# A perceiver layer with cross attention, gated linear attention and experts: one first norm instead of two, head norms by square root and reciprocal, weight splits three blocks ahead, and the turns of self attention ahead of the next scores

## The reference, cut to what matters

```python
def _ln(x, w, b):
    mu = jnp.mean(x, axis=-1, keepdims=True)
    var = jnp.mean(jnp.square(x - mu), axis=-1, keepdims=True)
    return (x - mu) * jax.lax.rsqrt(var + EPS) * w + b          # EPS = 1e-05

def _fp8_linear_pertensor(x, wq, w_scale, in_scale):
    xq = _div_clamp_fp8(x, in_scale)          # clip, bfloat16, then fp8 e4m3
    return jnp.einsum('bsi,oi->bso', xq * in_scale, wq) * w_scale

# x: (8, 64, 512); 16 heads of queries, 8 of keys and values, 128 wide
x1 = _layernorm(x)                            # (x - mean) / sqrt(var + 1e-5)
ln_out = _ln(x1, ln_w, ln_b)
q  = _ln(_fp8_linear_pertensor(ln_out, wq,  wq_scale,  q_in_scale).reshape(b, s, g, hpg, d), qln_w, qln_b)
qx = _ln(_fp8_linear_pertensor(ln_out, wqx, wqx_scale, qx_in_scale).reshape(b, s, g, hpg, d), qxln_w, qxln_b)
k  = _ln(_fp8_linear_pertensor(ln_out, wk,  wk_scale,  k_in_scale).reshape(b, s, g, d), kln_w, kln_b)
v  = _fp8_linear_pertensor(ln_out, wv, wv_scale, v_in_scale).reshape(b, s, g, d)
core = _gqa(q, k, v)                          # self attention, 64 positions a batch
# then cross attention of qx with 1601 context rows a batch, the output
# projection, x = x + ...; a gated delta-rule attention layer; a mixture of
# experts: none of them is touched by the change
```

## Time and profile before

| | before |
|---|---|
| median of 3 runs | 3088.67 us (3081.49 to 3090.84) |
| profiled execution | 3089.42 us |
| its span, first to last instruction | 3087.6 us |
| TensorE busy, share of the span | 2750.4 us, 89% |
| DVE busy | 1848.7 us, 60% |
| ACT busy | 1502.0 us, 49% |
| POOL busy | 535.5 us, 17% |
| TensorE busy in the first 320 us | 201.2 us, 63% |
| TensorE busy, 320 to 900 us | 560.0 us, 97% |

### The profile page before, as it was taken

One profiled execution on the slowest core, in us unless ns is written; L12 is line 12 of the kernel. 1 busy time (PEld: TensorE's weight loads), 2 busy tenths in 40 slices (PEclk: granted clock), 3 DMA queues, 4 the chain that ended last, 5 costly groups with the idle time before them and its releaser, 6 DMA issues.

```text
span 3087.6 us, 38294 instructions
## 1 busy us (share of the span) xinstructions
PE 2750.4 (89%) x13446; PEld 2223.8 (72%) x13446; DVE 1848.7 (60%) x4678; ACT 1502.0 (49%) x2880; POOL 535.5 (17%) x359
## 2 busy tenths in 40 slices
PE   4667999999999999999999999677998878886999
PEld 3556777778778687787787777555876778765887
DVE  6843744735636437446365373476858867466997
ACT  3652533524434326235244252233676466855776
POOL 3530200201102002011010020133333222102111
PEclk8886999999999999999999999878999989997999
DMA  2333401102003012021020020332666553418996
GB/s 85 96 89 111 120 2 48 51 4 70 27 9 89 4 38 61 4 62 35 5 87 11 22 66 3 127 109 75 164 179 167 161 124 76 141 69 337 380 374 242
DMA packets 246877, 303.06 MB, mean 98 GB/s; under 512 B 143896, under 2 KB 165016, under 8 KB 233376
## 3 DMA queue, kind: packets, MB, share of 16 engines
q1 hardware_dynamic: 243888, 296.36, 30.2%
q0 software_dynamic: 2800, 4.27, 0.6%
HBM read 259.48 MB, written 46.98 MB: 99 GB/s over the span
## 4 chain that ended last, share of the span: by engine, by line
PE 68%; DVE 16%; ACT 7%; issue 3%; DMA 2%; POOL 2%; SPq 2%; POOLq 0%; ACTq 0%; DVEq 0%
PE ps L103 17%; PE ps L105 16%; PE ps L104 16%; PE ps L690 5%; PE ps L707 3%; PE ps L672 2%; PE ps L737 2%; DVE tq L1138 2%; DVE lnw L787 1%; DVE lnw L1835 1%; DVE zz L1838 1%; POOL rs L345 1%; DVE cv L1802 1%; PE ps L728 1%; ACT pr L908 1%
## 5 line engine op out<-in xcount | busy, mean ns | idle before, releaser
L1017 POOL TENSOR_TENSOR lnw<-lnw,half 128x8 f32<-128x8 f32 (+1 forms) x104 | 170.7, 1642 | 1464.9 <-DVE lnw L792 1464.9
L103 PE MATMUL ps<-whf,cth 128*128 128x512 f32 (+1 forms) x832 | 340.1, 409 | 8.2 <-DVE ctl L509 4.8
L103 PE MATMUL ps<-cnh,pth 128*128 128x512 f32 (+1 forms) x832 | 331.3, 398 | 13.7 <-ACT kn L908 13.7
L105 PE MATMUL ps<-whf,ctl 128*128 128x512 f32 (+1 forms) x832 | 329.7, 396 | 0.0
L104 PE MATMUL ps<-wlf,cth 128*128 128x512 f32 (+1 forms) x832 | 329.2, 396 | 0.0
L105 PE MATMUL ps<-cnh,ptl 128*128 128x512 f32 (+1 forms) x832 | 325.3, 391 | 0.0
L104 PE MATMUL ps<-cnl,pth 128*128 128x512 f32 (+1 forms) x832 | 325.0, 391 | 0.0
L898 DVE TENSOR_SCALAR pc<-ps,sm 128x512 f32<-128x512 f32 x64 | 48.1, 751 | 318.2 <-PE ps L105 318.2
L2275 DVE TENSOR_TENSOR ml<-mr,mh 128x2048 fp32r<-128x2048 f32 x90 | 203.5, 2288 | 34.5 <-ACT mh L2219 34.5
L908 ACT ACTIVATE pr<-ps,lnw 128x128 f32<-128x128 f32 (+1 forms) x384 | 144.5, 457 | 162.0 <-DVE lnw L811 162.0
L939 ACT ACTIVATE pr<-ps,sm 128x1601 f32<-128x1601 f32 x64 | 102.6, 1603 | 247.4 <-DVE sm L831 217.3
(11 more groups left out here) (315 smaller groups left out, 6305.8 us busy)
## 6 DMA issues: line engine op xcount, KB each, us to landing
mr<-in_moe SPq DMA_DIRECT2D x90, 1024.0 KB, 7.2
ctr<-in_ctxt SPq DMA_DIRECT2D x96, 256.0 KB, 2.9
pr<-in_ctxn SPq DMA_DIRECT2D x96, 256.0 KB
wr<-in_wqkv SPq DMA_DIRECT2D x64, 256.0 KB, 2.9
wvf<-in_wattn SPq DMA_DIRECT2D x12, 1024.0 KB, 4.9
ca<-cat_d SPq DMA_DIRECT2D x8, 1024.0 KB, 5.7
pw<-in_wproj SPq DMA_DIRECT2D x8, 1024.0 KB, 8.3
qk_d<-cv SPq DMA_DIRECT2D x32, 256.0 KB, 3.2
```

Source lines behind the costliest of these rows:

```text
L103: pe.matmul(dst, lh, rh, start=first, stop=False)
L105: return pe.matmul(dst, ll, rh, start=False, stop=last)
L1017: po.tensor_tensor(rs[0:w, s, :], nv[0:w, s, :], half[0:w, 0:8], ALU.pow).then_inc(kx_rs, 1)
```

## The change

- The two first norms become one. The variance v of x goes to `nv` as v(1 + 1e-5) + 1e-10, whose power of minus one half is the product of both scalings; the second pass is no longer made.
- Head norms: ACT takes the square root of `nv1` (with a bias of 1e-5 from a new tile `eps5`) into `rs1`, DVE its reciprocal. POOL has no part in it.
- `split_weight_ac` becomes `scale_weight_ac` and `split_weight_ac`; both work for block j+3 in iteration j, where they were for j+2, and the scaling and the split stand on either side of ACT's half of `qn`. POOL's remainder is four instructions of 128x512. POOL's first split waits for the applied norm, its second for the first quantized input.
- Quantizing: `quantize_x_dv` moves behind DVE's half of `qn`, and `quantize_x_ac` from the start to the end of ACT's iteration.
- `project_pe` waits for the heads of block j-2 bank by bank instead of for all four.
- Self attention: TensorE turns pair i before the scores of pair i+1 (they came after), DVE computes the sums of pair i+1 before it copies pair i, and ACT copies `pT` of pair i before the exponent of pair i+1.

```diff
--- before.py
+++ after.py
@@ -140,6 +140,7 @@
         pT = sb1("pT", [128, 8, 128])
         am = sb1("am", [128, 2, 16])
         asum = sb1("asum", [128, 2, 16])
+        eps5 = sb1("eps5", [128, 1])
         s1.close()
 
         d_w, d_qx = sems("d_w", 2), sems("d_qx", 4)
@@ -174,7 +175,8 @@
                         sp.dma_start(qx_d[:, :, hd // 2, hd % 2, :].rearrange("b p s -> p b s"),
                                      qxs[:, n % 4, :].rearrange("p (b s) -> p b s", b=NB)).then_inc(d_qx[n % 4], 16)
 
-        def layer_norm_dv(dv, n):
+        def layer_norm_dv(dv):
+
 
             for i in range(4):
                 t = vs(dv.bn_stats(bns[:, i, 0, :], x0[:, i, :]))
@@ -182,8 +184,8 @@
                 dv.wait_ge(dv_step, t - 3 + i)
                 t2 = vs(dv.bn_aggr(mv[:, i, 0, :], bns[:, i, 0, :]))
             dv.wait_ge(dv_step, t2)
-            dv.tensor_scalar(nv[:, :, 0], mv[:, :, 0, 1], 1e-5, None, ALU.add).then_inc(ln_var, 1)
-            dv.wait_ge(ln_rs, n + 1)
+            dv.tensor_scalar(nv[:, :, 0], mv[:, :, 0, 1], 1.0 + 1e-5, 1e-10, ALU.mult, ALU.add).then_inc(ln_var, 1)
+            dv.wait_ge(ln_rs, 1)
             for i in range(4):
                 dv.tensor_scalar(x0[:, i, :], x0[:, i, :], mv[:, i, 0, 0:1], rs[:, i, 0:1],
                                  ALU.subtract, ALU.mult).then_inc(ln_done, 1)
@@ -212,10 +214,9 @@
         def s1_dv(dv):
             dv.memset(half[:, :], -0.5).then_inc(consts_set, 1)
             dv.memset(eps6[:, :], 1e-6).then_inc(consts_set, 1)
+            dv.memset(eps5[:, :], 1e-5).then_inc(consts_set, 1)
             dv.wait_ge(d_x, 16)
-            layer_norm_dv(dv, 0)
-            dv.wait_ge(ln_done, 4)
-            layer_norm_dv(dv, 1)
+            layer_norm_dv(dv)
             dv.wait_ge(d_vec, 16)
             for c in range(4):
                 dv.wait_ge(x_turned, c + 1)
@@ -241,13 +242,10 @@
                     for m in range(16):
                         tb = vs(dv.bn_aggr(mv1[:, s, m, :], bn1[:, s, m, :]))
                     dv.wait_ge(dv_step, tb)
-                    tb = vs(dv.tensor_scalar(nv1[:, s, :], mv1[:, s, :, 1], wsc, wsc, ALU.mult, ALU.mult))
+                    dv.tensor_scalar(nv1[:, s, :], mv1[:, s, :, 1], wsc, wsc, ALU.mult, ALU.mult).then_inc(hn_var, 1)
+                    dv.wait_ge(hn_rs, j + 1)
+                    tb = vs(dv.reciprocal(rs1[:, s, :], rs1[:, s, :]))
                     dv.wait_ge(dv_step, tb)
-                    dv.tensor_scalar(nv1[:, s, :], nv1[:, s, :], 1e-5, None, ALU.add).then_inc(hn_var, 1)
-                if j < 9:
-                    t = quantize_x_dv(dv, j // 3 + 1, j % 3, t)
-                if KIND[j] < 3:
-                    dv.wait_ge(hn_rs, j + 1)
                     tb = vs(dv.tensor_scalar(rs1[:, s, :], rs1[:, s, :], wsc, None, ALU.mult))
                     dv.wait_ge(dv_step, tb)
                     dv.scalar_tensor_tensor(nm1[:, s, :], mv1[:, s, :, 0], -1.0, rs1[:, s, :],
@@ -260,6 +258,8 @@
                             f = dv.tensor_scalar(qn[:, s, i, 128 * h:128 * h + 128], bank(b0 + i)[:, 128 * h:128 * h + 128],
                                                  mv1[:, s, m, 0:1], rs1[:, s, m:m + 1], ALU.subtract, ALU.mult)
                     f.then_inc(hn_dv, 1)
+                if j < 9:
+                    t = quantize_x_dv(dv, j // 3 + 1, j % 3, t)
 
         def quantize_x_ac(ac, k):
             if k >= 1:
@@ -268,37 +268,45 @@
                 f = ac.activation(yb1[:, c, :], lnT[:, c, :], ACT.Copy, scale=rsc[:, 4 * k + c:4 * k + c + 1])
             f.then_inc(quant_y, 1)
 
-        def split_weight_ac(ac, j):
+        def scale_weight_ac(ac, j):
             s, kind = j % 2, KIND[j]
             ac.wait_ge(d_w[s], 16 * (j // 2 + 1))
             for c in range(4):
                 t = cs(ac.activation(wraw[:, s, c, :], wraw[:, s, c, :], ACT.Copy,
                                      scale=vec[:, 8 + 4 * kind + c:9 + 4 * kind + c]))
+            return t
+
+        def split_weight_ac(ac, j, t):
             ac.wait_ge(ac_step, t)
             if j >= 2:
                 ac.wait_ge(proj, 4 * (j - 2) + 4)
-            ac.activation(wh[:, s, :, :], wraw[:, s, :, :], ACT.Copy).then_inc(w_high, 1)
+            ac.activation(wh[:, j % 2, :, :], wraw[:, j % 2, :, :], ACT.Copy).then_inc(w_high, 1)
 
         def s1_ac(ac):
             ac.wait_ge(d_vec, 16)
-            split_weight_ac(ac, 0)
+            t = scale_weight_ac(ac, 0)
+            split_weight_ac(ac, 0, t)
             ac.wait_ge(lnT_done, 4)
-            ac.wait_ge(consts_set, 4)
+            ac.wait_ge(consts_set, 5)
             quantize_x_ac(ac, 0)
-            split_weight_ac(ac, 1)
+            t = scale_weight_ac(ac, 1)
+            split_weight_ac(ac, 1, t)
+            t = scale_weight_ac(ac, 2)
+            split_weight_ac(ac, 2, t)
             ac.wait_ge(d_row, 16)
             for j in range(12):
                 s, kind, b0 = j % 2, KIND[j], 4 * (j % 2)
-                if j < 9 and j % 3 == 0:
-                    quantize_x_ac(ac, j // 3 + 1)
                 if j + 1 >= 10 and j + 1 < 12:
                     g0, b1 = 4 * (j + 1 - 10), 4 * ((j + 1) % 2)
                     for i in range(4):
                         ac.wait_ge(proj, 4 * (j + 1) + i + 1)
                         ac.activation(vv[:, i, g0:g0 + 4, :], bank(b1 + i).rearrange("p (g d) -> p g d", g=4), ACT.Copy,
                                       scale=row[:, 67:68]).then_inc(vv_out, 1)
-                if j + 2 < 12:
-                    split_weight_ac(ac, j + 2)
+                if kind < 3:
+                    ac.wait_ge(hn_var, j + 1)
+                    ac.activation(rs1[:, s, :], nv1[:, s, :], ACT.Sqrt, bias=eps5[:, 0:1]).then_inc(hn_rs, 1)
+                if j + 3 < 12:
+                    t = scale_weight_ac(ac, j + 3)
                 if kind < 3:
                     ac.wait_ge(hn_nm, j + 1)
                     if j >= 2:
@@ -309,6 +317,9 @@
                             f = ac.activation(qn[:, s, i, 128 * h:128 * h + 128], bank(b0 + i)[:, 128 * h:128 * h + 128],
                                               ACT.Identity, scale=rs1[:, s, m:m + 1], bias=nm1[:, s, m:m + 1])
                     f.then_inc(hn_ac, 1)
+                if j + 3 < 12:
+                    split_weight_ac(ac, j + 3, t)
+                if kind < 3:
                     wcol, bcol = ((24, 25), (28, 29), (26, 27))[kind]
                     for h in range(4):
                         src = bank(b0 + h).rearrange("p (b s) -> p b s", b=NB)
@@ -325,26 +336,25 @@
                         ac.wait_ge(turned, 4 * j + h + 1)
                         ac.activation(dst, src, ACT.Identity, scale=vec[:, wcol:wcol + 1],
                                       bias=vec[:, bcol:bcol + 1]).then_inc(heads_out, 1)
+                if j < 9 and j % 3 == 0:
+                    quantize_x_ac(ac, j // 3 + 1)
 
         def split_weight_po(po, j):
             s = j % 2
             po.wait_ge(w_high, j + 1)
-            po.tensor_tensor(wl[:, s, :, :], wraw[:, s, :, :], wh[:, s, :, :].bitcast(fp32),
-                             ALU.subtract).then_inc(w_split, 1)
+            for c in range(4):
+                f = po.tensor_tensor(wl[:, s, c, :], wraw[:, s, c, :], wh[:, s, c, :].bitcast(fp32), ALU.subtract)
+            f.then_inc(w_split, 1)
 
         def s1_po(po):
             po.wait_ge(consts_set, 1)
-            for n in range(2):
-                po.wait_ge(ln_var, n + 1)
-                po.tensor_tensor(rs[:, :, 0], nv[:, :, 0], half[:, 0:4], ALU.pow).then_inc(ln_rs, 1)
+            po.wait_ge(ln_var, 1)
+            po.tensor_tensor(rs[:, :, 0], nv[:, :, 0], half[:, 0:4], ALU.pow).then_inc(ln_rs, 1)
+            po.wait_ge(ln_done, 4)
             split_weight_po(po, 0)
-            split_weight_po(po, 1)
-            for j in range(12):
-                if KIND[j] < 3:
-                    po.wait_ge(hn_var, j + 1)
-                    po.tensor_tensor(rs1[:, j % 2, :], nv1[:, j % 2, :], half[:, 0:16], ALU.pow).then_inc(hn_rs, 1)
-                if j + 2 < 12:
-                    split_weight_po(po, j + 2)
+            po.wait_ge(quant_x, 1)
+            for j in range(1, 12):
+                split_weight_po(po, j)
 
         def project_pe(pe, j):
             s, kind, b0 = j % 2, KIND[j], 4 * (j % 2)
@@ -352,9 +362,9 @@
             pe.wait_ge(quant_x, kind + 1)
             if j < 2:
                 pe.wait_ge(lnT_done, 4)
-            else:
-                pe.wait_ge(heads_out, 4 * (j - 2) + 4)
             for i in range(4):
+                if j >= 2:
+                    pe.wait_ge(heads_out, 4 * (j - 2) + i + 1)
                 for c in range(4):
                     lhs = xq[:, kind % 2, c, 128 * i:128 * i + 128]
                     pe.matmul(bank(b0 + i), lhs, wh[:, s, c, :], start=c == 0, stop=False)
@@ -363,7 +373,7 @@
 
         def s1_pe(pe):
             pe.wait_ge(d_cst, 16)
-            pe.wait_ge(ln_done, 8)
```

(17 more changed lines are left out.)

## The result

The changed kernel takes 3043.41 us (median of 4, 3039.68 to 3045.46), the one before 3085.63 (median of 4): ratio 0.9861, 95% interval 0.9841 to 0.9881. That is 42.2 us less; the forecast was 43.8 less for the profiled execution, and a median of 3045. The profiled execution took 3042.77 us (before 3089.42), its span is 3041.0.

The account below looks back on a forecast made before the run. Before the scores, POOL's power and DVE's `rs1` scaling, waiting for POOL, were taken as the bound, not TensorE. Scores 32.4 earlier plus self attention 11.4 gave 43.8 off 3089.42: 3045.6, median 3045, range 3030 to 3063.

Parts of the forecast that it names:

- The opening: Up to the first projection: 10.2 us from the norm, 4.3 from the `xq` collision; start at 26.85 instead of 41.34.
- The square root, and the table: Head norms and exponent: two table loads of 1.28 us on the path; a drain would make the sum 2.8 worse.
- The two kinds of block: Time between square roots: 20.0 us for blocks 0, 3, 6, which wait for `quant_y`; 10.8 to 12.3 for the others.
- POOL's pieces: Short blocks: scaling of `rs1` and `nm1` wait for POOL's pieces, 1.5 us, in one block of two.
- Rival 1: Blocks: POOL's next piece always goes first and starves DVE; 8 to 9 us worse, 3054; chance 0.15.
- Heads bank by bank: Projections starting per bank: gain under 2 us a block in TensorE's own order, with TensorE not last.
- Rival 3: Projections and turns: TensorE stays at 1.2 GHz, scores start 3 us later than before; 3090; chance 0.03.
- Self attention: First scores to ACT's last copy: 60.8 us instead of 72.15, gain 11.4, bounds 6 and 18; 12.8 a pair.
- Rival 2: TensorE stays warm (2.4 GHz): 7 us better in self attention, 2 to 4 in stage one; 3035; chance 0.14.
- Rival 4: Weight loads come late: binds from a landing of 10 us, undoes all 44 us from 26 on; chance 0.02.
- Rival 5: Blocks 0, 3, 6: the late `quant_y` is not waited for, each 9 us shorter; 3025; chance 0.03.
- two table loads a block: Head norms on ACT: activation tables loaded twice in each block; 3071; chance 0.03.

Follow-up runs that it names:

- p_norm: The kernel before with the one first norm alone, POOL's first split waiting for the applied norm: 3074.8 us, ratio 0.9965.
- u_xq: The changed kernel without POOL's wait for the first quantized input ahead of the split of block 1: 3041.0 us, ratio to the kernel before 0.9847.
- p_head: The kernel before with square root and reciprocal for the head norms alone: 3048.2 us, ratio 0.9882.
- u_quant: The changed kernel with `quantize_x_ac` back at the start of ACT's iteration: 3016.4 us, ratio to the kernel before 0.9770.
- u_piece: The changed kernel with POOL's remainder of a weight block in one 128x2048 instruction again: 3048.3 us, ratio to the kernel before 0.9869.
- u_heads: The changed kernel, but a projection waits for all four heads of block j-2: 3057.3 us, ratio to the kernel before 0.9912.
- u_self_pe: The changed kernel with only TensorE's old self-attention order (scores of pair i+1, then turn of pair i): 3026.6 us, ratio to the kernel before 0.9808.
- s_simple: The kernel before with one first norm, square root and reciprocal, and projections starting bank by bank: 3035.8 us, ratio 0.9831.

## Why the prediction was right, point by point

- **The opening.** Right to 0.2: first projection at 27.03 (26.85). The 10.2 for the norm is shown by p_norm (10.1). The 4.3 for the collision at `xq` was gained, but with the pieces the wait is hardly needed for it (u_xq gives back 1).
- **The square root, and the table.** The power's removal is worth 29.5 alone, the most of the single edits, and 17.6 at the end of all edits; the prediction had no term for it alone. The first table load is on the path (1.28 between `nv` and the square root). The second is not, a term that I had at 1.28: it was issued at 189.21, right behind the last value copy, and ACT then idled 5.3 us. Of the drain that the prediction quoted none shows: the square root starts 0.02 behind the load. The prediction's "about 25 later" for block 8 is misread: the power of block 8 started at 175.38 before, which is 18 later than the forecast's 157.6. So of the 33.7 us only 18.8 are gained at block 8. A part of the other 15 is ACT's weight work (2.55 and 1.91), which stood between the square root and `qn` of block 9 in p_head, and in the kernel before between the value copies and that `qn`; with the weights three blocks ahead block 9 has none left, and its `qn` starts 1.1 behind the square root instead of 4.6 (p_head).
- **The two kinds of block.** Forecast 20.0 and 10.8 to 12.3; measured 19.4 to 19.7 and 11.2 to 11.9. The wait for `quant_y` is shown by u_quant: the scores start 21.5 later for it. That the change holds back part of its own gain was in the forecast as the 20.0.
- **POOL's pieces.** Right in size (the two short blocks of a group lose 1.3 and 2.0 us to POOL in the first two groups, forecast 1.5), wrong in detail: every short block collides and not one of two, `nv` collides too, which I had left out, and so does block 0. And it is not the pieces that freed `rs` and `nm` (u_piece). Rival 1, DVE starved, is out by u_xq. The Trainium skill (SBUF — State Buffer, Who interferes with whom) names copies, casts and `tensor_scalar`, where their operands allow it, as well as instructions with two inputs in SBUF as those that can contend with GpSimd; the trace agrees as far as it goes: `nv`, `rs` and `nm` were held up, and the reciprocal, at 0.25 in all ten blocks, with POOL at its split beside six of them, never was.
- **Heads bank by bank.** Here the reasoning failed: "gain under 2 us a block in TensorE's own order, and TensorE is not last here". The sum was not touched, because it started the projections per bank, but the edit is worth 17.6 us. TensorE is not last here only because its gaps are short; in u_heads ACT waits for it in five blocks, 17.0 us in all. That the longer gap is what lowers the clock is read from the order of the rows; no run changed the gap alone. Rival 3, TensorE at 1.2 GHz throughout, is out: the projection of block 4 ran at a granted clock of 1.00.
- **Self attention.** 62.5 for 60.8, and two errors partly cancel in it, which is luck: up to the first turn 10.35 for 11.6 (the table load), the three pairs 41.5 for 38.4, the rest 10.6 for 10.8. A pair takes 13.8, above the 13.5 that I had as the upper end of that chain: turn (1.97), scores (5.5 to 5.7) and maximum to probabilities are last, at a clock that is low for a part of it. TensorE's own loop of 14.6 is not what binds. Rival 2, a TensorE that stays warm, did not come true in the changed kernel; u_self_pe's warm pair of 9.25 came by another order.
- **Loads.** Rival 4 is out: beside the first, ACT waited for one weight load in the changed kernel, 0.81 us for block 2 in the opening. Rival 5 is out by DVE's wait of 7.55 us ahead of `yb`, and two table loads a block are out by ACT's rows.

## What to carry to other kernels

When work is moved to the end of an engine's iteration, look for the other engine that consumes it in the same iteration: here that one placement cost 21.5 us and took two lines to mend. Judge a reordering by each engine's order alone: in self attention the orders of DVE and ACT brought the gain and TensorE's cost 15. An edit that only shortens gaps on an engine that is not last may still carry the stage: here, with a gap of 3.1 us instead of 1.1, the next projection took 9.1 us instead of 7.6, and the other engines waited for it.

## What was not expected of the hardware

POOL instructions of 1.25 us in a row let DVE in between them: DVE waited 0.94 us in front of `xq` where one instruction of the same work cost it 4.3. In block 3 of the changed kernel it gets in three times during one split: `nv`, `rs` and `nm` end at 83.15, 84.41 and 85.66, 1.26 and 1.25 apart, each with one of POOL's pieces:

```profile
80.60 5.03 POOL L346 TENSOR_TENSOR wlf<-wvf,whf 128x512 fp32r<-128x512 f32 x4 [7.44 <-ACT whf L283]
```

A table load can be issued long before the data of the instruction that it serves is there (189.21, with the exponent at 195.76), but in front of the first square root it waited (40.12, 0.08 behind `nv`). In p_head and s_simple the load for the first square root did not wait either (ACT's timeline of p_head):

```profile
43.92 1.28 ACT L304 ACT_TABLE_LOAD   x1
54.24 0.31 ACT L304 ACTIVATE rs<-nv,eps 128x16 f32<-128x16 f32 x1 [9.04 <-DVE nv L246]
```

The programs differ in what stands directly ahead. Where the load waited for `nv`, two waits follow each other there, `ac.wait_ge(d_row, 16)` and `ac.wait_ge(hn_var, 1)`; in p_head and s_simple ACT's scaling of `yb` stands between the two, and the exponent has one wait alone. So here 1.28 us may hang on where a wait that is long satisfied stands; no run moved that wait alone.
